# The inverted residual section with its depthwise convolution as 32x32 diagonal tiles on four image rows

## What is computed

```python
def _bn(x, g, b, m, v):
    scale = (g * lax.rsqrt(v + EPS)).reshape(1, -1, 1, 1)
    shift = (b - m * g * lax.rsqrt(v + EPS)).reshape(1, -1, 1, 1)
    return x * scale + shift
h = jnp.einsum('oc,bchw->bohw', w1, x)                 # 48 -> 288 channels
h = jax.nn.relu(_bn(h, g1, b1, m1, v1))
h = lax.conv_general_dilated(h, wd, (1, 1), ((1, 1), (1, 1)), feature_group_count=288, ...)   # 3x3 depthwise
h = jax.nn.relu(_bn(h, gd, bd, md, vd))
h = jnp.einsum('oc,bchw->bohw', w2, h)                 # 288 -> 48 channels
h = _bn(h, g2, b2, m2, v2)
return x + h
```

## Time and profile before

| | before |
|---|---|
| median of three runs | 2199.33 us |
| span of the profiled execution | 2196.4 us |
| TensorE busy | 1961.0 us, 89% |
| VectorE busy | 1781.7 us, 81% |
| ScalarE busy | 1306.5 us, 59% |
| GpSimdE busy | 861.6 us, 39% |
| the section inverted_residual | 1560.6 to 2196.4 us |
| HBM traffic, whole program | 83.90 MB read, 37.75 MB written |

### The profile page before, as it was taken

One profiled execution on the slowest core, in us unless ns is written; L12 is line 12 of the kernel. 1 busy time (PEld: TensorE's weight loads), 2 busy tenths in 40 slices (PEclk: granted clock), 3 DMA queues, 4 the chain that ended last, 5 costly groups with the idle time before them and its releaser, 6 DMA issues. The chain is left out here.

```text
span 2196.4 us, 33549 instructions
## 1 busy us (share of the span) xinstructions
PE 1961.0 (89%) x9170; PEld 1366.2 (62%) x9170; DVE 1781.7 (81%) x3407; ACT 1306.5 (59%) x2355; POOL 861.6 (39%) x700
## 2 busy tenths in 40 slices
PE   6979099999999996199999999985299999999998
PEld 5535067777777772177777777761176667666675
DVE  5539778888888885588888888875599999999997
ACT  1116067777777775477777777766266556665664
POOL 2010056565665650256656566540322222222221
PEclk9989599999999998599999999997599999999999
DMA  2778500000000006500000000008411111111110
GB/s 78 251 198 166 133 26 23 21 23 23 23 23 22 23 14 110 149 24 23 23 21 23 23 23 23 22 12 129 143 37 43 43 43 39 38 38 42 43 36 22
DMA packets 82573, 122.04 MB, mean 56 GB/s; under 512 B 13856, under 2 KB 33168, under 8 KB 82544
## 3 DMA queue, kind: packets, MB, share of 16 engines
q1 hardware_dynamic: 82544, 121.70, 21.7%
HBM read 83.90 MB, written 37.75 MB: 55 GB/s over the span
## 5 line engine op out<-in xcount | busy, mean ns | idle before, releaser
L668 PE MATMUL gates_l<-xh_l,w_hi_l 112*112 112x512 f32 x3072 | 819.3, 402 | 104.3 <-DVE keep_l L730 104.3
L668 PEld LDWEIGHTS gates_l<-xh_l,w_hi_l 112*112 112x112 f32 x3072 | 537.4, 175 | 302.6 <-issue 105.1
L644 POOL TENSOR_TENSOR xh_l<-xf_l,xh_l 48x512 fp32r<-48x512 f32 x256 | 359.3, 1403 | 280.8 <-ACT xh_l L687 280.4
L668 PE MATMUL gates_l<-xh_l,w_lo_l 112*112 112x512 f32 x1536 | 449.6, 401 | 0.0
L1298 DVE SCALAR_TENSOR_TENSOR b_acc_v<-b_hidden_v,b_wd,b_acc_v 128x512 f32<-128x512 f32 x512 | 381.4, 745 | 0.0
L639 POOL TENSOR_TENSOR xh_l<-hs,xh_l 48x512 fp32r<-48x512 f32 x254 | 303.4, 1194 | 173.6 <-DVE hs L759 173.6
L668 PEld LDWEIGHTS gates_l<-xh_l,w_lo_l 112*112 112x112 f32 x1536 | 269.6, 175 | 97.9
L1145 PE MATMUL b_ps<-b_hidden_t,b_diag_hi 128*128 128x512 f32 x1152 | 302.7, 407 | 0.0
L699 ACT ACTIVATE gate_if_l<-gates_l 112x512 f32<-112x512 f32 x256 | 153.0, 598 | 245.3 <-PE gates_l L668 245.3
L739 DVE TENSOR_TENSOR keep_l<-gate_if_l,cell_l 48x512 f32<-48x512 f32 x256 | 175.5, 685 | 140.6 <-ACT gate_if_l L699 140.6
L1145 PEld LDWEIGHTS b_ps<-b_hidden_t,b_diag_hi 128*128 128x128 f32 x1152 | 212.4, 189 | 64.9 <-issue 12.7
(11 more groups left out here) (146 smaller groups left out, 1975.5 us busy)
## 6 DMA issues: line engine op xcount, KB each, us to landing
xf_l<-rows SPq DMA_DIRECT2D x256, 96.0 KB, 2.1
hs<-rows SPq DMA_DIRECT2D x32, 384.0 KB, 10.7
rows<-hs SPq DMA_DIRECT2D x32, 384.0 KB, 5.0
b_xs<-rows SPq DMA_DIRECT2D x128, 96.0 KB, 2.2
xr<-in_x_rows SPq DMA_DIRECT2D x24, 256.0 KB, 2.7
xc<-in_x_cols SPq DMA_DIRECT2D x24, 256.0 KB, 2.9
mixed<-stage SPq DMA_DIRECT2D x24, 256.0 KB, 3.0
edged<-stage SPq DMA_DIRECT2D x24, 256.0 KB, 3.2
```

Source lines behind the costliest of these rows:

```text
L644: pool.tensor_tensor(xh[far[d]:far[d] + C, d, s, 1, :, 1:W + 1], xf[far[d]:far[d] + C, s, :].rearrange("p (b w) -> p b w", b=B), xh[far[d] ...
L668: mm = nc.tensor.matmul(ps[d][m][0:K, :], weight[:, d, m, t, :], xh[0:K, d, s, part, :, t:t + W], start=(first and t == 0), stop=(last and ...
```

## The change

inverted_residual is written anew; the sections before it stay. Scales are folded into the weights, so that only biases are left. All data are plain float32: the rounded copies, their low parts and the hardware loops are gone. The unit is a block of four image rows (BLK = 4, 16 blocks), written out one after another.

Sets 0 and 1 are both convolved by TensorE. For each tap, 16 float32 matmuls of 32x32 diagonal weights run over 512 columns: channel quarter i of the input (partitions 32i to 32i + 31) and output place j (partitions 32j to 32j + 31) serve image row r = (j - i) mod 4, and each of the four image rows has a PSUM bank of its own, `b_dw`. In bank r the channel quarters stand rotated by r places, so biases and reduction weights have an order per row. Set 2's taps are nine instructions of 128x512 on VectorE for four rows. ScalarE squashes rows 0 and 1 of a block, VectorE rows 2 and 3.

```diff
+                def expand(k, n):
...
+                    if n < EPB - 1:
+                        g, p = divmod(n, 2)
+                        for h in range(2):
+                            rows = slice(h * HALF, h * HALF + C)
+                            mm = nc.tensor.matmul(banks(e)[h][:, :], w1s[rows, g * P:(g + 1) * P], xs[rows, s, p, :],
+                                                  start=True, stop=True)
...
-                    for part, d in ((0, diag_hi), (0, diag_lo), (1, diag_hi)):
-                        if part:
-                            pe.wait_ge(rows_lo, y + 2)
-                        for t in range(9):
-                            dy, dx = t // 3 - 1, t % 3
-                            mm = nc.tensor.matmul(ps2[s % 2][:, :], d[:, t, :],
-                                                  hidden_t[:, slot(s + dy), part, :, dx:dx + W],
-                                                  start=(d is diag_hi and part == 0 and t == 0), stop=(part == 1 and t == 8))
...
+                    for n, (dy, dx) in enumerate(ORDER):
+                        for i in range(BLK):
+                            for j in range(BLK):
+                                r = (j - i) % BLK
+                                y = BLK * k + r + dy
+                                if not 0 <= y < H:
+                                    continue
+                                last = n == 8 or (n == 5 and BLK * k + r == H - 1)
+                                mm = nc.tensor.matmul(dw[r][j * Q:(j + 1) * Q, :], diag[i * Q:(i + 1) * Q, g, 3 * dy + 3 + dx, :],
+                                                      hid[g][i * Q:(i + 1) * Q, y % RING, :, dx:dx + W],
+                                                      start=(n == 0), stop=last, skip_group_check=True)
...
+                for k in range(NBLK):
+                    more = k + 2 < NBLK
+                    depthwise(k, 0)
+                    if more:
+                        expand(k + 2, 0)
+                    if k:
+                        if k == 1:
+                            pe.wait_ge(w2_ready, 1)
+                        reduce_main(k - 1, 0)
+                        reduce_rest(k - 1, 0)
+                    if more:
+                        expand(k + 2, 1)
+                    depthwise(k, 1)
...
+                for k in range(NBLK):
+                    more = k + 2 < NBLK
+                    squash(k, 0)
+                    if more:
+                        keep(k + 2, 0, (0, 1))
+                        keep(k + 2, 1, (0, 1))
+                    squash(k, 1)
+                    if more:
+                        keep(k + 2, 2, (0, 1))
+                        keep(k + 2, 3, (0, 1))
+                        keep(k + 2, 4, (0, 1))
...
+                def scale_of(tmp, variance, gain, n, rows=P):
+
+                    pool.tensor_scalar(tmp[0:rows, 0, :], variance, EPS, 0.0, ALU.add, ALU.add).then_inc(steps, 1)
+                    pool.wait_ge(steps, n + 1)
+                    pool.tensor_tensor(tmp[0:rows, 1, :], tmp[0:rows, 0, :], half_power[0:rows, 0:tmp.shape[2]],
+                                       ALU.pow).then_inc(steps, 1)
...
+                pool.wait_ge(loaded, 160)
+                scale_of(t1, bn1[:, 1, :], bn1[:, 0, :], 1, K)
+                pool.wait_ge(steps, 4)
+                pool.tensor_tensor(w1s[:, :], w1[:, :], t1[:, 2, :], ALU.mult).then_inc(w1_ready, 1)
...
+                            nxt = nc.vector.scalar_tensor_tensor(acc_r[:, :, :], src, weight, acc_r[:, :, :], ALU.mult, ALU.add)
```

More of the change, by code:

```diff
@@ L912, in inverted_residual @@
     K = HALF + C
-    RING = 4
+    Q = 32
+    SETS = 2
+    BLK = 4
+    NBLK = H // BLK
+    RING = 16
+    XRING = 5
+    EPB = 5
+    PRO = 2 * EPB
+    ORDER = [(dy, dx) for dy in (0, -1, 1) for dx in range(3)]
     with ctx:
@@ new lines, in by_dve, with banks, targets, view @@
+        def by_dve(e):
+            return min(e + 1, PRO)
+        def banks(e):
+            return ys if e < PRO and e % 2 else ex
+        def targets(k, n):
+            if n < EPB - 1:
+                g, p = divmod(n, 2)
+                return [(hid[g][:, (BLK * k + 2 * p + h) % RING, :, 1:W + 1], g) for h in range(2)]
+            first = BLK * k + 1
+            return [(hid_r[:, first + h:first + h + 3:2, :, 1:W + 1], 2) for h in range(2)]
+        def view(bank, n):
+            if n < EPB - 1:
+                return bank[:, :].rearrange("p (b w) -> p b w", w=W)
+            return bank[:, 0:2 * QB * W].rearrange("p (r b w) -> p r b w", r=2, w=W)
@@ L1108, in _ @@
-                step(0)
-                with pool.Fori(1, H // RING - 1) as k:
-                    step(k)
-                step(H // RING - 1, last=True)
+                pool.memset(half_power[:, :], -0.5).then_inc(steps, 1)
+                def scale_of(tmp, variance, gain, n, rows=P):
[3 more added lines that the diff above has]
+                                       ALU.pow).then_inc(steps, 1)
+                    pool.wait_ge(steps, n + 2)
+                    return pool.tensor_tensor(tmp[0:rows, 2, :], tmp[0:rows, 1, :], gain, ALU.mult).then_inc(steps, 1)
@@ L1255, in _, with keep @@
-                step(0, first=True)
-                with act.Fori(1, H // RING - 1) as k:
-                    step(k)
-                step(H // RING - 1, last=True)
-                affine_rows(H // 2 - 1, 1)
+                def keep(k, n, halves):
+                    e = EPB * k + n
+                    act.wait_ge(expanded, e + 1)
+                    for h in halves:
+                        dst, g = targets(k, n)[h]
+                        nc.scalar.activation(dst, view(banks(e)[h], n), ACT.Relu, bias=bias_h[:, g:g + 1]).then_inc(kept_a, 1)
@@ L1303, in finish @@
-                def finish(j, s, earlier):
-                    dve.wait_ge(affine, j + 1)
-                    dve.wait_ge(r_in[s], 32 * earlier + 32)
-                    wait(dve, stored[s], 32 * earlier)
-                    nc.vector.tensor_tensor(o[:, s, :], scaled[:, s, :], res[:, s, :], ALU.add).then_inc(final, 1)
-                def step(k):
-                    for u in range(RING):
-                        depthwise(k * RING + u, u)
-                        if u == 1 and not (isinstance(k, int) and k == 0):
-                            finish(k * 2 - 1, 1, k - 1)
-                        if u == 3:
-                            finish(k * 2, 0, k)
@@ new lines, in _, with keep @@
+                for side in (0, W + 1):
+                    nc.vector.memset(hid_r[:, :, :, side:side + 1], 0.0).then_inc(pads, 1)
+                for y in (0, H + 1):
+                    nc.vector.memset(hid_r[:, y, :, 1:W + 1], 0.0).then_inc(pads, 1)
+                def keep(k, n):
+                    e = EPB * k + n
+                    dve.wait_ge(expanded, e + 1)
+                    dst, g = targets(k, n)[1]
+                    nc.vector.tensor_scalar(dst, view(banks(e)[1], n), bias_h[:, g:g + 1], 0.0, ALU.add, ALU.max
+                                            ).then_inc(kept_d, 1)
@@ new lines, in _ @@
+                for k in range(NBLK):
+                    taps(k, range(0, 3))
+                    squash(k, 0)
+                    taps(k, range(3, 9))
+                    squash_rest(k)
+                    if k:
+                        if k == 1:
+                            dve.wait_ge(biases, 4)
+                        finish(k - 1, 0)
+                    squash(k, 1)
+                    if k:
+                        finish(k - 1, 1)
+                for p in range(2):
+                    finish(NBLK - 1, p)
```

520 lines of the change are left out of this document (229 added, 291 removed).

## The result

The changed kernel takes 2122.32 us (median of 4 runs, 2118.29 to 2211.3) against 2201.44 of the kernel before on the same chip. The ratio is 0.9646, with a 95% interval of 0.9626 to 0.9665. 2083 had been predicted, faster, so the sign was right and the gain too large: 79 us instead of 116. One run in four of each kernel was slow as a whole (2288.14 and 2211.3) and is left out of the ratio. The profiled execution has a span of 2122.2 us, 42 over the predicted 2080.

The account below looks back on a forecast made before the run. TensorE and VectorE were taken as both full before, TensorE alone after. First depthwise at 1647.5 plus 432.4 (blocks 351, 26.3, 43.8; end 11.3) gave a 2080 span; with 2.9 added, 2083 us. Range 2035 to 2330, own range 2025 to 2140.

Parts of the forecast that it names:

- The bound: Rewritten section: TensorE sets a block's time; VectorE's 12.1 us and ScalarE's 10.5 hide under 27.0; GpSimdE idle in the loop.
- Row groups overlap: Depthwise matmuls: tiles in four row groups and four column groups run at once, 0.86 us a round instead of 3.44.
- row groups don't overlap: Rival for the depthwise: only column groups overlap, a round 3.44 us, a call 31.3, time 2873; chance 0.09.
- A round at 0.86, a call at 8.1: Depthwise: 16 matmuls of one tap cost two records, 0.86 us; nine rounds plus small extras make a call 8.1 us.
- The block between the calls: TensorE outside a block's two depthwise calls: 4.7 us before the second and 6.1 after, in a block of 27.0.
- The start: Section start: GpSimdE's power over 288 columns takes 59 us on the path, putting the first depthwise near 1647.5.
- The sum: Whole kernel: first depthwise at 1647.5 plus 432.4 us of blocks and end gives a span of 2080, predicted time 2083.
- Rounds don't overlap: Rival for the depthwise: a record must finish before its tile's next, round near 1.29 us, call 12.0, time 2208; chance 0.11.
- Supply or half the tiles: Rival for the depthwise: instruction supply or eight overlapping tiles at most, round 1.7 us, call 15.7, time 2326; chance 0.18.
- The range: Whole kernel's time: 2035 to 2330 us, leaving out the last rival and little of the others; forecast's own range 2025 to 2140.
- expansion halves one after another: Expansion matmuls in the blocks: if the two row halves don't overlap, 48 us more, counted in the own range's upper end.
- strided reading: Depthwise input: strided reading at L1145's surplus, 11% of 7.7 us, some 20 us more in the own range's upper end.

Follow-up runs that it names:

- blocks 4 to 7: Changed kernel with taps 2 to 9 on four tiles only, chosen by block; these blocks use one row group and four column groups; whole run 2123.84 us.
- version with parameters first: Changed kernel with w1's scale moved into ScalarE's activation and SyncE issuing the eight small parameter transfers before the first images; 2082.09 us.
- the other order inside a round: Changed kernel with each round's 16 matmuls reordered: neighbours in different row and column groups, writing one PSUM bank; 2119.77 us.
- VectorE relieved: Changed kernel with VectorE's taps 2 to 9 of set 2 on 128 of the 512 columns; 2118.63 us.

## Why the prediction came out as it did

**The bound.** Right. TensorE is busy for 99% of the steady stretch, VectorE's work is hidden (110.49 of 300 us, and taking a third of it away changes nothing), and GpSimdE has nothing in the loop. A block holds 11.12 us of VectorE and 8.23 of ScalarE, where 12.1 and 10.5 had been forecast.

**Row groups overlap.** Right, and it was the step on which the case hung. The rival "row groups don't overlap" (2873) is what the version without tiles nearly is (2793); four row groups in one column group ran at 0.858 a round.

**A round at 0.86, a call at 8.1.** This is the step that failed, in its size. The first two rounds of a call and all rounds of 4 or 8 tiles are at that price. With 16 tiles in turn a round is 1.04. The prediction put the start of 16 tiles into the call once, as 0.15 us; something of this size, 0.18 us, is paid in every round from the third on. Against the call of eight tiles (8.15 us) the six intervals that follow cost 1.1 us, and the last round, 1.66 us to the next instruction instead of 1.26, costs 0.4. A call is 9.68 us, 1.58 over the forecast; 32 calls make 50.6 us. By the figure of the Trainium skill, "TensorE: Matmul & The Clock Gate", part 3, the prediction had 1.30 us for a round. The measured round lies between the two prices. If one tile alone costs what an untiled matmul does, 16 x 0.864 / 1.04 is 13.3 times faster than one after another, where the Trainium skill has 10.6. The prediction named the figure and gave its price, but the sum took nothing from it.

**The block between the calls.** Right: 4.86 + 6.02 = 10.88 us against 4.7 + 6.1 = 10.8. An expansion with its row halves at once is 1.06 us, against 0.96. After the second call the forecast had a chain of ScalarE of 6.1 us with the reduction hidden in it. ScalarE does come last there, but only by 0.34 us; TensorE's own work is the other 5.68.

**The start.** Right in kind, 8 us too late in size. The power takes 46.4 us and not 59: 0.161 us a column, where the slope from 1 to 6 columns gave 0.204 and the one from 1 to 2 columns 0.153; the lower bound, 44, was the better one. The section's own start was 3.6 us later than before. So the first depthwise is at 1639.9 instead of 1647.5.

**The sum again, with what was measured.** 2080 - 7.6 for the start, + 50.6 for the calls, + 1.4 for one call at a granted clock of 0.86 (1668.13, 11.05 us), less 1.4 for the four calls at the upper and lower edge of the image, which have 12 matmuls fewer: 2123, and the span is 2122.2.

**The rivals.** "Rounds don't overlap" (1.29 a round) erred on the round as much as the forecast did on the other side, 0.21 to 0.25 us against 0.18 to 0.21; its 2208 is further from the measured time than 2083. "Supply or half the tiles" (1.7) erred three times as much. More than eight tiles do overlap. The supply rival had a true core that the prediction's rows didn't show: at 0.62 to 0.65 us a round the instructions no longer come fast enough, in the run with half the columns. In the changed kernel the supply is just enough; its calls repeat to 0.01 us but for two (rows of 9.87 and 10.04 us where the others have 9.75). The Trainium skill, "TensorE: Matmul & The Clock Gate", part 1, gives about 62 ns of handling per matmul with hardware decode off. By that a round of 32 records would be 1.98 us. It is not seen in this kernel, where they take 1.04 us.

**The range.** 2035 to 2330 held 2122.3. The forecast's own range, 2025 to 2140, did too, and that was partly luck. Its upper end was made of expansion halves one after another (48) and of strided reading (20), which add up to 2151 and not 2140. Neither happened: an expansion took 1.06 us, and rounds of four and eight tiles took 0.858. The loss came from a term that the range didn't have, the rounds of 16 tiles, and the start, 7.6 us too long, hid a part of it.

## What to carry to other kernels

Count what small concurrent matmuls cost by rounds, and size the round from the longest run of them that a trace shows: four and eight tiles took no longer here than one untiled matmul (0.86 us), sixteen lost a fifth of a microsecond in each round from the third on. Look at what a rewrite puts ahead of its loop as closely as at the loop: one GpSimdE instruction over 288 columns took back 46 of the 119 us that the loop gained (16 x (4 x 9.42 - 30.23)), and the same scale on 3 columns, used by ScalarE, took 0.88 us there and 0.18 us in each block. When a section's start is moved forward, look at TensorE's granted clock there before counting the gain.

## What the runs showed that was not expected

- Four tiles out of a single row group didn't hold the full clock (granted 0.65 to 0.79 in blocks 4 to 7, 0.67 in the stretch shown), while four tiles spread over four row groups held 1.00, with the same number of matmuls and columns in a call. TensorE was busy for 98% of both stretches shown.
- After the section's idle start the clock rises and then falls again: for 3.4 us in the changed kernel, and twice for 6.8 us in the version with parameters first. Warming TensorE brought the rise forward and didn't remove the falls. The number and length of the falls vary without the start having changed: one of 3.4 us with the other order inside a round, two of 3.4 and 6.8 us with VectorE relieved. In the traces of the changed kernel and nine of its versions there are 14, and each begins inside a wait of TensorE for ScalarE of 1.4 to 1.7 us or within 1.8 us behind one (in the changed kernel the wait ends at 1667.36 and the clock falls at 1667.71). In the blocks behind, where TensorE waits 0.34 us at most, the clock of the changed kernel holds for 450 us. But not every such wait is followed by a fall, and no run takes the waits away, so that they are the cause is not shown.
- A float32 matmul costs some 260 bytes of instructions by the estimate above. Written out without a loop, 16 tiles in turn at 0.62 to 0.65 us a round ran out of them, with stops of up to 2.1 us that ended behind a transfer.
- Rounds of 12, 14 and 15 tiles are slow for two, three and four rounds and then return to 0.858. What makes them slow, and what lets them recover, is open.
